# In the last head group of an attention layer, VectorE adds two heads of each pair of key blocks and GpSimd the other two, from the eleventh pair on

## The reference

```python
x = x + attention(layernorm(x), Wq, Wk, Wv, Wo)   # causal, rotary q and k, softmax(q k / sqrt(32)) v
x = x + ffn(layernorm(x))                         # x W + b, plus a rank-16 LoRA of 8 experts, the top 2 gated
```

## Time and profile before

| what | us |
|---|---|
| median of 3 runs | 1527.97 |
| lowest and highest | 1527.58, 1528.42 |
| the profiled execution, its own time | 1526.67 |
| its span in the trace | 1524.9 |
| busy in the span: TensorE / VectorE / ScalarE / GpSimd | 1502.9 / 1132.9 / 756.5 / 891.8 |

### The profile page before, as it was taken

One profiled execution on the slowest core, in us unless ns is written; L12 is line 12 of the kernel. 1 busy time (PEld: TensorE's weight loads), 2 busy tenths in 40 slices (PEclk: granted clock), 3 DMA queues, 4 the chain that ended last, 5 costly groups with the idle time before them and its releaser, 6 DMA issues.

```text
span 1524.9 us, 24726 instructions
## 1 busy us (share of the span) xinstructions
PE 1502.9 (99%) x9056; PEld 977.4 (64%) x9056; DVE 1132.9 (74%) x2280; ACT 756.5 (50%) x1543; POOL 891.8 (58%) x597
## 2 busy tenths in 40 slices
PE   8999999999999999999999999999999989999999
PEld 6888887755555555555555555555555547777777
DVE  7766666899777777877777877877777677666665
ACT  4222222255666666656656666666665673232222
POOL 2323322577778778778788788797797721121111
PEclk9999999999999999999999999999999999999999
DMA  6655785757449458467467565754845363223311
GB/s 213 234 188 186 229 268 192 212 127 172 96 91 211 92 114 189 91 132 168 98 132 157 121 139 123 155 123 108 186 102 136 83 153 112 83 83 107 140 57 55
DMA packets 120404, 215.84 MB, mean 142 GB/s; under 512 B 12504, under 2 KB 45784, under 8 KB 113112
## 3 DMA queue, kind: packets, MB, share of 16 engines
q1 hardware_dynamic: 102384, 136.20, 32.7%
q0 software_dynamic: 8064, 58.72, 18.8%
q10 hardware_dynamic: 9840, 19.40, 3.6%
HBM read 96.23 MB, written 58.72 MB: 102 GB/s over the span
## 4 chain that ended last, share of the span: by engine, by line
PE 91%; DVE 5%; DMA 1%; ACT 1%; issue 1%; POOL 0%; SPq 0%; DVEq 0%; POOLq 0%; ACTq 0%
PE a_mx L275 16%; PE a_av L1140 16%; PE a_st L1127 16%; PE p_pair L558 11%; PE f_wo_ps L1491 6%; PE f_out_ps L1551 5%; PE p_v L570 5%; PE a_sum L275 3%; PE a_sum L1162 2%; DVE a_part L290 2%; PE a_sum L1170 2%; PE f_out_ps L1566 1%; PE f_mid_ps L1491 1%; ACT a_probs L1228 1%; PE a_mx L279 1%; PE f_tr_ps L1510 1%
## 5 line engine op out<-in xcount | busy, mean ns | idle before, releaser
L1228 ACT ACTIVATE a_probs<-a_st 128x512 f32<-128x512 f32 (+2 forms) x1244 | 573.9, 546 | 343.6 <-PE a_st L1127 336.5
L290 DVE TENSOR_REDUCE a_part<-a_mx 128x1 f32<-128x512 f32 (+1 forms) x766 | 490.4, 680 | 81.7 <-PE a_mx L275 72.7
L1076 POOL TENSOR_TENSOR a_pair<-a_probs 128x1024 f32<-128x1024 f32 (+2 forms) x224 | 401.8, 1835 | 16.4 <-DMA a_gather<-a_pair 6.2
L1076 POOL TENSOR_TENSOR a_gather<-a_probs 128x1024 f32<-128x1024 f32 x76 | 179.9, 2388 | 97.2 <-ACT a_probs L1228 97.2
L412 POOL TENSOR_TENSOR p_rot<-p_mul 128x1024 f32<-128x1024 f32 x32 | 88.3, 2761 | 186.2 <-DVE p_mul L787 186.1
L1484 POOL TENSOR_TENSOR f_x<-f_x,f_bias 128x512 f32<-128x512 f32 x32 | 40.3, 1292 | 200.1 <-DVE f_xn L1704 200.1
L1140 PE MATMUL a_av<-a_probs,a_v 128*32 128x512 f32 (+3 forms) x1280 | 139.8, 537 | 2.5 <-POOL a_probs L1057 2.5
L1140 PE MATMUL a_av<-a_probs,shared 128*32 128x512 f32 (+3 forms) x1280 | 140.1, 537 | 0.0
L293 DVE CUSTOM_DVE_ANT_0 a_mx<-a_mx,f_ctx 128x512 f32<-128x512 f32 (+1 forms) x161 | 98.6, 630 | 51.8 <-PE a_mx L275 51.8
L1057 POOL TENSOR_SCALAR_AFFINE_SELECT a_probs<-a_probs 128x512 f32<-128x512 f32 x128 | 89.0, 760 | 54.5 <-ACT a_probs L1228 51.7
L1127 PE MATMUL a_st<-a_q_stack,a_k_stack 98*128 98x512 f32 (+3 forms) x287 | 101.4, 371 | 1.1 <-DMA a_q_stack<-a_neg_rows 1.1
(11 more groups left out here) (256 smaller groups left out, 3038.5 us busy)
## 6 DMA issues: line engine op xcount, KB each, us to landing
a_gather<-a_pair POOLq DMA_DIRECT2D x56, 1024.0 KB, 7.2
qk_scratch<-p_rot_hi SPq DMA_DIRECT2D x32, 512.0 KB, 3.1
qk_scratch<-p_rot_lo SPq DMA_DIRECT2D x32, 512.0 KB, 4.1
a_k_stack<-qk_scratch SPq DMA_DIRECT2D x60, 256.0 KB, 8.1
a_q_first<-qk_scratch SPq DMA_DIRECT2D x48, 256.0 KB, 6.3
a_third<-qk_scratch SPq DMA_DIRECT2D x36, 256.0 KB, 5.5
v_scratch<-p_v_st SPq DMA_DIRECT2D x32, 256.0 KB, 7.0
ctx_scratch<-a_ctx_st SPq DMA_DIRECT2D x32, 256.0 KB, 3.1
```

Of the source, the lines that this page charges most:

```text
L290: dve.tensor_reduce(found, scores.rearrange("p (h n) -> p h n", n=width), AX.X, ALU.max).then_inc(self.max_done, 1)
L1076: pool.tensor_tensor(place[:, h:h + 2, q0:TT], probs[:, s % RING, h:h + 2, q0:TT], probs[:, (s + 1) % RING, h:h + 2, q0:TT], ALU.add).then ...
L1228: act.activation(probs[:, s % RING, h, q0:TT], score_bank(g, HG * s + h)[:, q0:TT], ACT.Exp, scale=SCORE_SCALE).then_inc(exp_done, 1)
```

## The change

GpSimd and VectorE share the additions of pairs 10 to 19 of the last group. VectorE adds heads 0 and 1 of each pair, GpSimd heads 2 and 3. As both count on the same semaphore, each of them first waits until both halves of the pair before are counted.

```diff
@@ add_pairs (GpSimd) @@
-                    if not (g == GROUPS - 1 and p >= NO_ITEMS):
-                        wait_place_of_pair(pool, g, p)
-                        place = place_of_pair(p)
-                        for h in range(0, HG, 2):
-                            pool.wait_ge(exp_done, exps(g, s + 1, h + 1))
-                            pool.tensor_tensor(place[:, h:h + 2, q0:TT], probs[:, s % RING, h:h + 2, q0:TT],
-                                               probs[:, (s + 1) % RING, h:h + 2, q0:TT], ALU.add).then_inc(pair_added, 1)
+                    shared_add = g == GROUPS - 1 and p >= NO_ITEMS
+                    if shared_add:
+                        pool.wait_ge(pair_added, 2 * (NPAIR * g + p))
+                    wait_place_of_pair(pool, g, p)
+                    place = place_of_pair(p)
+                    for h in range(2 if shared_add else 0, HG, 2):
+                        pool.wait_ge(exp_done, exps(g, s + 1, h + 1))
+                        pool.tensor_tensor(place[:, h:h + 2, q0:TT], probs[:, s % RING, h:h + 2, q0:TT],
+                                           probs[:, (s + 1) % RING, h:h + 2, q0:TT], ALU.add).then_inc(pair_added, 1)
@@ add_pair (VectorE) @@
+                dve.wait_ge(pair_added, 2 * (NPAIR * g + p))
                 wait_place_of_pair(dve, g, p)
-                place = place_of_pair(p)
-                for h in range(0, HG, 2):
-                    dve.wait_ge(exp_done, exps(g, s + 1, h + 1))
-                    dve.tensor_tensor(place[:, h:h + 2, q0:TT], probs[:, s % RING, h:h + 2, q0:TT],
-                                      probs[:, (s + 1) % RING, h:h + 2, q0:TT], ALU.add).then_inc(pair_added, 1)
+                dve.wait_ge(exp_done, exps(g, s + 1, 1))
+                dve.tensor_tensor(place_of_pair(p)[:, 0:2, q0:TT], probs[:, s % RING, 0:2, q0:TT],
+                                  probs[:, (s + 1) % RING, 0:2, q0:TT], ALU.add).then_inc(pair_added, 1)
```

## The result

| | before | after |
|---|---|---|
| median of 6 runs, us | 1528.20 (1527.47 to 1529.11) | 1532.56 (1531.30 to 1534.45) |
| the profiled execution: time, span, us | 1526.67, 1524.9 | 1531.30, 1529.6 |
| first scores of unit 3 | 1218.04 | 1218.01 |
| values of step 36 | 1249.87 | 1254.23 |
| first product of `finish` | 1257.93 | 1262.40 |

The kernel became slower by 4.36 us. The ratio is 1.003, with a 95% interval of 1.002 to 1.004. The two profiled executions are alike up to unit 3, and 4.5 of the 4.7 us between the spans arise between 1218 and 1262.

A forecast was written before the change was run, and what follows sets the result against it. TensorE bounds the kernel, waiting on additions, joins and landings before the mask of step 36: + 3.1 us there, + 0.1 in the tail, taken as + 3.1 on 1527.97, giving 1531.1 us; range 1529.3 to 1532.9.

The forecast's parts named there:

- third rival: GpSimd's join issue held up by VectorE's casts, or another subtraction going ahead: + 1 to + 2.5 us on top, chance 0.17.
- The turns: VectorE's and GpSimd's halves exclude each other: a pair of 1024-column halves costs 3.48 us in place of 2.36.
- additions side by side: Second rival, shared pairs: the engines overlap freely, additions of 2.4 and 1.2 us at once; 1528.3 us, chance 0.07.
- casts did wait: First rival, VectorE's casts: they don't exclude GpSimd's additions, 1.4 to 1.5 us less, 1529.6 us, chance 0.11.
- The landing of join 15: DMA after pair 15: lands 5.5 us after join 14, at 1247.6 in place of 1245.5, part of the loss hidden.
- The tail: From the values of step 36 to `finish`: 8.2 us in place of 8.06, so + 0.1.
- pairs 10 to 12 and the division: Early shared pairs and GpSimd's division, which ends at 1231 in place of 1227.2: nothing lost, as TensorE needs them later.
- pair 13: Halves until 1229.8 in place of 1229.4, then division, cast and subtraction in turn, done by about 1231.5: nothing lost.

The follow-up runs named there:

- Tiny halves: Kernel after with GpSimd's or VectorE's half of pairs 10 to 19 cut to 8 columns a head: - 1.16 or + 1.51 us against before.
- clock_kept: Kernel after with 16 filling products on TensorE ahead of the values of step 36: + 4.61 us against before.
- only_10_13: Kernel after with additions shared in pairs 10 to 13 alone, VectorE making all others: + 1.97 us against before.
- only_14_17: Kernel after with additions shared in pairs 14 to 17 alone, VectorE making all others: + 3.48 us against before.
- vector_half_tiny: Kernel after with VectorE's half of pairs 10 to 19 cut to 8 columns a head, GpSimd's whole: + 1.51 us against before.
- direct_split: Kernel before with last-group pairs 16 and 17 summed by TensorE without joins, VectorE's large split moved to after pair 15, small ones too: 1525.93 against 1529.13 us.

## Why the prediction was right, and where it was off

The forecast was + 3.1 us, it became + 4.4. That is inside the range of 1529.3 to 1532.9, but above the 1530.3 to 1532.1 that the forecast's own terms gave, and where the third rival was put (1532.1 to 1533.6), whose mechanism didn't occur. So the range held partly because it was widened for that rival, which is luck. The 4.4 us by which the values of step 36 are late are 2.3 us from the later landing of join 14, about 1.0 from the slower landing of join 15 and 1.1 from the turns in pair 17 (3.42 in place of 2.36 us). Step by step:

- **The turns** were right to 0.2 us as far as the join of pair 15. Joins 14 and 15 were forecast for 1235.2 and 1239.8 and issued at 1235.34 and 1240.01; pair 17 took 3.4 us from its landing, forecast 3.5. Tiny halves show that it's GpSimd's duration added to VectorE's, not the hand-over. Two of the three rivals fell with the trace: additions side by side didn't become shorter than their sum, and casts did wait (2.62 us).
- **The landing of join 15** is the term that was mis-sized. I took 5.5 us after join 14's, from the four joins of before. It was 6.6 us (1242.2 to 1248.8), and nothing of the loss was hidden by the DMA's own queue: issued 3.0 us later than before, the join landed 3.3 us later. These 1.1 us pass to the additions of pair 17, the mask and `finish` undiminished: 1.1 of the 1.3 us by which the forecast was short. I had allowed up to 5.8 us for it, from a single pattern of gaps, which was too narrow. What the term left out is shown below.
- **The tail** was forecast at 8.2 us from the values of 36 to `finish`, and took 8.17, but not for my reason. I had expected the wait ahead of pair 18's sum to stay. It is gone, since the halved clock stretched TensorE's own work over it; clock_kept shows the wait again at the full clock, with `finish` 0.2 us earlier. That the number fits is luck.
- **The third rival** didn't occur. Joins weren't held up at their issue: 0.87 to 0.91 us each, the last of them under the long cast; and no other subtraction went ahead of the mask of step 36 (the masks of 1253.52 took 1.24 us, and the large subtraction waited). By the Trainium skill (SBUF — State Buffer, the "DVE blocks DMA" trap) the last join would have had to wait for the end of that cast. The traces disagree: it was issued in 0.91 us with the cast running, 0.04 more than the others, and in no run here was a join held up.
- **What I costed at nothing**, pairs 10 to 12 and the division, was nothing: `finish` didn't wait for it. But pair 13, which I gave no loss of its own, starts the delay: VectorE's cast waits behind GpSimd's half, and only_10_13 loses 2.0 us without one shared pair after it.

**Why join 15 lands late** is seen in the DMA packets of the traces. A join is 128 packets of 8 KB and 16 of under 512 B, and these small ones come last; I read each as the end of one of sixteen parts. For join 15 of the kernel after, the stretches 1246.6 to 1246.9 and 1248.4 to 1248.6 have 15 small packets and 1:

```profile
DMA packets 16, 0.01 MB, mean 28 GB/s; under 512 B 15, under 2 KB 15, under 8 KB 15
...
DMA packets 2, 0.01 MB, mean 41 GB/s; under 512 B 1, under 2 KB 1, under 8 KB 1
```

So fifteen parts of the join are done 4.9 us after those of join 14, and one comes 1.65 us behind the others. Before, the last one of join 15 was 0.4 us behind. In both traces one packet of another queue, of the kind "instruction", comes into these microseconds. It is 16 KB, takes 0.95 us, and while it lasts 15 packets of the joins are under way in place of 16. After, it starts in 1244.96 to 1244.99, with join 15 under way; before, in 1245.00 to 1245.03, together with the last small packet of join 15 and so behind that join:

```profile
q8 instruction: 1, 0.02, 198.3%
...
DMA packets 2, 0.02 MB, mean 546 GB/s; under 512 B 1, under 2 KB 1, under 8 KB 1
...
q8 instruction: 1, 0.02, 197.1%
```

Twelve of the thirteen kernels fit this. In five of them join 15 landed 5.5 to 5.6 us after join 14. There the instruction packet starts within 0.02 us of the last small packet of join 15, which is 0.3 to 0.5 us behind the fifteenth. In seven, those whose join 15 was issued 0.7 us or more later than in before, it starts 0.9 to 5.5 us ahead of the last small packet, which is 1.3 to 1.7 us behind the fifteenth, and the landing comes 6.3 to 7.2 us after that of join 14. The fifteenth keeps its pace in all twelve, 4.9 to 5.2 us after that of join 14. The longest, 7.0 to 7.2 us, are the three (only_10_13, only_14_17, vector_half_tiny) in which the last small packet directly follows the instruction packet; there the landing is counted 1.1 us after it, elsewhere 0.3 to 0.5. The thirteenth kernel, direct_split, is the exception: 6.3 us with all sixteen parts late together. There seventeen packets of the join that start between 1243.3 and 1244.6 take about 1.26 us in place of 0.63, after another transfer of 1 MB (`f_ctx`) was issued at 1240.23.

So the 5.5 us of before were those of a join that ended just ahead of the instruction packet, and a later join doesn't. This is read from where the packets lie; no run moved the instruction packet by itself. A part of the delay stays open too: the packet takes 0.95 us, and the last part of the join is up to 1.65 us late.

## What to carry to other kernels

Halving an addition over VectorE and GpSimd made it longer here, where both halves read SBUF: 1.2 and 2.4 us gave 3.4 to 3.5, and a fast cast in VectorE's queue waited for its turn too. Look for overlaps of the two engines elsewhere in the trace of before, which price this in advance. A transfer in the path deserves the same care: its landing is that of its slowest part, so look what else is in the DMA queues where it will come to lie. And follow the chain behind the edit: here the gain lay in taking work out of the chain of joins and a large instruction out of the queue ahead of it (direct_split), not in more engines for the additions.

## What the runs showed of the hardware that was not expected

- Of two instructions in a row on GpSimd, the second kept VectorE waiting as well: both masks of 1253.52 (1.24 us) ran at full speed while a subtraction that had started at 1253.43 took 3.49 us.
- Accumulating joins of 1 MB that overlap landed 4.2 to 7.2 us apart. Where one packet of 16 KB of the instruction queue, 0.95 us long, came ahead of the last part of join 15, it was 6.3 to 7.2 us, and 5.5 to 5.6 where it came right behind.
- With 2.5 to 2.6 us of idle time ahead of the values of step 36, TensorE's clock fell to half in two traces and not in that of before; it stayed low for about 7 us and cost 1.0 to 1.1 us where TensorE was what the end waited for. In the kernel after it cost 0.2 us, as TensorE would have waited.
